# Conditional 1x1 mix plus low-rank update: where TensorE waits in its instruction stream

## The chip, the cores and the metric

The kernel runs on one core of one Trainium2 chip. The metric is the device time of one execution in microseconds (us). Five engines run their own instruction streams and meet only at semaphores: TensorE (PE in the profile; its weight loads are PEld), VectorE (DVE), ScalarE (ACT), GpSimd (POOL) and SyncE (SP), which issues all the transfers here.

## The reference

`x` holds 64 batches of 128 channels by 2048 time steps, in float32. Each batch has a number from 0 to 15 that picks a 128x128 matrix, and a number from 4 to 50 that picks a low-rank adapter.

```python
W = weights[condition]                            # 16 matrices, 128 x 128
x = x + jnp.einsum('bct,bcd->bdt', x, W)          # mix of channels
Bx = jnp.einsum('bni,bri->bnr', x, B[adapter_ids])   # rank 16, over time
out = jnp.einsum('bnr,bor->bno', Bx, A[adapter_ids])
x = x + out                                       # scaling is 1
```

So every batch needs three products: a mix of the channels, a sum over time to rank 16, and a product back to all time steps, with two additions of the input around them.

## The kernel before

A batch is one 128 x 2048 tile. It is worked in four **units** of 512 columns. Batches go in **rounds** of two (`ROUND`), rounds in **turns** of two (`BODY` = 4 batches), so every buffer of a batch exists four times and the two rounds of a turn are of kind 0 and kind 1. 16 turns make 64 batches; turn 0 and the last turn are written out, the 14 between are a hardware loop.

For a batch b the work is:

- POOL adds the identity to the picked matrix (`m_sel`, L215; semaphore `m_picked`), so that the mix gives x + x W at once.
- **mix** (L374): 16 matmuls on PE, one bank of PSUM for each unit; `f_made` counts units. ACT copies each unit out of its bank into `ft` (L262; `copied`).
- **z** (L390): 16 matmuls with 16-column weights from `ab_in` and `ft` as moving data. The four chunks of a unit write four 32-row strips of bank 0 or 1; `z_done` at the end. ACT takes strips 0 and 2 out of the bank, DVE strips 1 and 3 (L269, L309; `z_taken_act`, `z_taken_dve`). POOL adds the four parts, ACT copies the sum to three more groups of rows (`z_placed`).
- **low** (L408): 16 matmuls with 16-row weights from `at`, which DVE makes by transposing half of `ab_in` (L325; `a_turned`). They run in four chunks; a chunk writes 128 columns in each of four banks. `low_done` comes with the last chunk. DVE then adds bank and `ft` for each unit into `x_out` (L316; `added`), and SP stores the tile.

Every matmul in float32 is issued in two pieces, so a stage of 16 matmuls shows 32 pieces in the trace.

PE's order is written out by hand. A round with batches b and b+1 runs mix(b), mix(b+1), z(b), z(b+1), low(b-2), low(b-1). The banks come round: the mix of a round begins in the banks that low of the first batch used in the round before it (`LOW_BANKS`, `F_BANKS`), so its first unit waits for the first `added` of that batch (L371). low of the second batch uses banks 0 and 1, in which z was summed, and so waits for all takes of z(b+1) (L403).

In the kernel before, each stage has its waits in front of its first matmul: `mix_units` at L364 to L371, `sum_z` at L381 to L387, `add_low_rank` at L397 to L404. Where a count depends on the loop's register, the wait is held by a register instruction of its own ahead of the matmul, or by the matmul's first weight load.

The last two batches are written out in another order: mix(62), z(62), low(60), mix(63), low(61), z(63), low(62), low(63). DVE's order at the end is: the adds of batches 58 and 59, the transposes of 62 and 63, the takes of z(62), the adds of 60, and so on.

## Time and profile before

| | us |
|---|---|
| median of 3 runs | 394.99 (393.74 to 397.9) |
| the profiled execution's own time | 394.86 |
| its span, first to last instruction | 393.0 |
| PE busy | 374.7 (95%) |
| PE weight loads busy | 352.8 (90%) |
| ACT busy | 238.5 (61%) |
| DVE busy | 230.2 (59%) |
| POOL busy | 113.2 (29%) |
| share of the DMA queue q1 | 96.3% of 16 engines, 152.19 MB |

Busy time is the time in which at least one instruction of the engine is in work; for PE it includes the stretch in which a matmul drains through the array. The profile also has a chain of waits (who released whom), a timeline, and for each transfer the time from issue to landing.

### The profile page before, as it was taken

How to read it: one execution, taken by the hardware profiler on the slowest of the kernel's cores; microseconds unless marked ns; L12 is line 12 of the kernel's file. 1: busy time of each engine (PE TensorE's matmuls, PEld its weight loads, DVE VectorE, ACT ScalarE, POOL GpSimd, SP SyncE). 2: the span in 40 equal slices, each digit the busy share in tenths (PEclk: the TensorE clock that was granted, in tenths of full speed). 3: DMA queues.
4: the chain of work that ended last, by engine and by line, in shares of the span. 5: the costliest groups of instructions: out<-in, count | busy, mean ns of one | idle time of the engine just before them, and what ended most of it. 6: DMA issues, size and time to landing. Idle time of an engine off the chain costs nothing.

```text
span 393.0 us, 16867 instructions
## 1 busy us (share of the span) xinstructions
PE 374.7 (95%) x6164; PEld 352.8 (90%) x6164; DVE 230.2 (59%) x445; ACT 238.5 (61%) x580; POOL 113.2 (29%) x263
## 2 busy tenths in 40 slices
PE   8789999999999999999999999999999999999971
PEld 8779999999999999999999999999999999999861
DVE  0127655567755556775555677555567765556752
ACT  2366665666666666666666666666666666566541
POOL 1033332223333222333322233332223333222310
PEclk9899999999999999999999999999999999999995
DMA  5998999999999999999999999999999999999547
GB/s 199 402 385 332 379 404 409 408 410 411 412 411 416 410 413 404 417 412 408 413 398 420 409 416 412 407 414 410 413 411 418 404 409 411 416 407 391 243 178 268
DMA packets 28815, 152.37 MB, mean 388 GB/s; under 512 B 3201, under 2 KB 3458, under 8 KB 12546
## 3 DMA queue, kind: packets, MB, share of 16 engines
q1 hardware_dynamic: 28802, 152.19, 96.3%
q8 instruction: 9, 0.15, 0.1%
q14 instruction: 4, 0.03, 0.0%
HBM read 85.07 MB, written 67.11 MB: 387 GB/s over the span
## 4 chain that ended last, share of the span: by engine, by line
PE 92%; DMA 2%; issue 1%; DVE 1%; SPq 1%; ACT 1%; POOL 1%; ACTq 0%; POOLq 0%; DVEq 0%
PE bank L374 59%; PE bank L408 17%; PE bank L390 16%; DMA x_in<-in_x 2%; DVE x_out L316 1%; POOL z_pair L224 0%; DMA ids<-in_ids 0%; DVE z_part L309 0%; SPq L138 0%; ACT x_out L300 0%; ACT z_all L274 0%; SPq L135 0%; SPq L139 0%; POOL z_all L229 0%; ACT ft L262 0%
## 5 line engine op out<-in xcount | busy, mean ns | idle before, releaser
L374 PE MATMUL bank<-m_sel,x_in 128*128 128x128 f32 x2048 | 240.5, 278 | 5.0 <-DMA x_in<-in_x 2.4
L374 PEld LDWEIGHTS bank<-m_sel,x_in 128*128 128x128 f32 x2048 | 233.7, 193 | 10.5 <-DVE x_out L316 3.2
L262 ACT COPY ft<-bank 128x512 f32<-128x512 f32 x256 | 146.0, 586 | 62.4 <-PE bank L374 60.2
L316 DVE TENSOR_TENSOR x_out<-bank,ft 128x512 f32<-128x512 f32 x253 | 154.4, 683 | 21.2 <-PE bank L408 21.2
L224 POOL TENSOR_TENSOR z_pair<-z_part 16x128 f32<-16x128 f32 x128 | 54.8, 444 | 212.8 <-DVE z_part L309 194.5
L309 DVE COPY z_part<-bank 16x128 f32<-16x128 f32 x128 | 36.7, 287 | 119.1 <-PE bank L390 117.1
L274 ACT COPY z_all<-z_all 16x128 f32<-16x128 f32 x192 | 56.9, 296 | 48.8 <-POOL z_all L229 45.8
L408 PE MATMUL bank<-z_all,at 16*128 16x128 f32 x2048 | 69.8, 283 | 2.6 <-DVE x_out L316 2.5
L408 PEld LDWEIGHTS bank<-z_all,at 16*128 16x128 f32 x2048 | 63.3, 188 | 9.7 <-issue 9.5
L390 PE MATMUL bank<-ft,ab_in 128*16 128x128 f32 x2048 | 65.7, 274 | 0.8 <-issue 0.8
L390 PEld LDWEIGHTS bank<-ft,ab_in 128*16 128x16 f32 x2048 | 51.4, 96 | 9.8 <-issue 4.2
L269 ACT COPY z_part<-bank 16x128 f32<-16x128 f32 x128 | 32.8, 256 | 33.6 <-PE bank L390 32.0
L325 DVE STREAM_TRANSPOSE at<-ab_in 128x512 f32<-128x512 f32 x64 | 41.5, 687 | 15.2 <-DMA ab_in<-in_lora 15.2
L215 POOL TENSOR_TENSOR m_sel<-w_all,ident 128x128 f32<-128x128 f32 x62 | 28.3, 456 | 40.4 <-PE bank L374 24.7
L229 POOL TENSOR_TENSOR z_all<-z_pair 16x128 f32<-16x128 f32 x64 | 28.5, 445 | 7.4 <-POOL z_pair L224 4.5
L416 PE MATMUL bank<-ident 128*128 128x128 f32 x20 | 4.6, 429 | 1.6 <-POOL ident L208 1.6
L416 PEld LDWEIGHTS bank<-ident 128*128 128x128 f32 x20 | 4.3, 331 | 1.6 <-POOL ident L208 1.6
L300 ACT COPY x_out<-bank 128x512 f32<-128x512 f32 x3 | 1.6, 594 | 2.3 <-PE bank L408 2.3
L236 POOL TENSOR_TENSOR m_sel<-w_first,ident 128x128 f32<-128x128 f32 x2 | 0.9, 453 | 7.0 <-DMA w_first<-in_weights 7.0
L262 ACT ACT_TABLE_LOAD x1 | 1.3, 1283 | 0.8 <-PEq L468 0.8
L208 POOL TENSOR_SCALAR_AFFINE_SELECT ident<-ident 128x128 f32<-128x128 f32 x1 | 0.3, 292 | 0.2 <-POOL ident L206 0.2
L206 POOL MEMSET ident<- 128x128 f32 x1 | 0.2, 204 | 0.3 <-POOLq L468 0.3
(5 smaller groups left out, 0.4 us busy)
## 6 DMA issues: line engine op xcount, KB each, us to landing
x_in<-in_x SPq DMA_DIRECT2D x63, 1024.0 KB, 11.8
out<-x_out SPq DMA_DIRECT2D x63, 1024.0 KB, 9.9
ab_in<-in_lora SPq DMA_DIRECT2D x64, 256.0 KB, 10.1
w_all<-in_weights SPq DMA_DIRECT2D x1, 1024.0 KB, 8.5
out<-x_out SPq DMA_DIRECT2D x4, 256.0 KB, 4.8
x_in<-in_x SPq DMA_DIRECT2D x2, 256.0 KB, 3.4
x_in<-in_x SPq DMA_DIRECT2D x1, 512.0 KB, 4.6
w_first<-in_weights SPq DMA_DIRECT2D x2, 64.0 KB, 2.7
```

Source lines behind the costliest of these rows:

```text
L215: nc.gpsimd.tensor_tensor(m_sel[k][:], w_all[:, cond, :], ident[:], ALU.add).then_inc(m_picked, 1)
L224: nc.gpsimd.tensor_tensor(z_pair[i][:], parts[2 * i][:], parts[2 * i + 1][:], ALU.add).then_inc(z_paired, 1)
L229: nc.gpsimd.tensor_tensor(z_all[k][rows_of_unit(0), :], z_pair[0][:], z_pair[1][:], ALU.add).then_inc(z_summed, 1)
L262: nc.scalar.copy(ft[k][u][:], bank[f_bank_of(kind, i, u, final)][:]).then_inc(copied, 1)
L269: nc.scalar.copy(z_part[i][c][:], rows_of_z(z_bank, c)).then_inc(z_taken_act, 1)
L274: nc.scalar.copy(z_all[k][rows_of_unit(u), :], z_all[k][rows_of_unit(0), :]).then_inc(z_placed, 1)
L309: nc.vector.tensor_copy(z_part[i][c][:], rows_of_z(z_bank, c)).then_inc(z_taken_dve, 1)
L316: nc.vector.tensor_tensor(x_out[k][:, UNIT * u:UNIT * (u + 1)], bank[banks[u]][:], ft[k][u][:], ALU.add).then_inc(added, 1)
L325: nc.vector.transpose(at[k][:], blocks).then_inc(a_turned, 1)
L374: last = nc.tensor.matmul(to[:, P * c:P * (c + 1)], x_in[k][:, UNIT * u + P * c:UNIT * u + P * (c + 1)], m_sel[k][:], start=(c == 0), stop ...
L390: last = nc.tensor.matmul(rows_of_z(z_bank, c), ab_in[k][:, first:first + RANK], ft[k][u][:, P * c:P * (c + 1)], start=(u == 0), stop=(u = ...
L408: last = nc.tensor.matmul(bank[banks[u]][:, P * c:P * (c + 1)], at[k][rows, js, :].rearrange("r j i -> r (j i)"), z_all[k][rows, :], start ...
```

## The change

Only PE's stream is changed; its matmuls and their order stay. The three stage functions become `mix_unit`, `sum_unit` and `low_chunk`, which hold almost no waits, and five `ask_for_...` functions hold the waits. They are called ahead of the last unit or chunk of a stage for what the next stage needs. Some waits are dropped because another covers them: `ab_loaded` and `z_summed` (covered by `a_turned` and `z_placed`) and two of the waits for `added`.

```diff
-            def sum_z(k, b, turns, z_bank, freed, taken):
-                pe.wait_ge(ab_loaded[k], 16 * turns)
-                pe.wait_ge(copied, UNITS * (b + 1))
-                if live(freed):
-                    pe.wait_ge(added, freed)
-                if live(taken):
-                    pe.wait_ge(z_taken_act, 2 * taken)
-                    pe.wait_ge(z_taken_dve, 2 * taken)
...
-            def add_low_rank(k, b, banks, freed, taken, own=False):
-                pe.wait_ge(a_turned, b + 1)
-                pe.wait_ge(z_summed, b + 1)
-                pe.wait_ge(z_placed, (UNITS - 1) * (b + 1))
-                if live(freed):
-                    pe.wait_ge(added, freed)
-                if live(taken):
-                    pe.wait_ge(z_taken_act, 2 * taken)
-                    pe.wait_ge(z_taken_dve, 2 * taken)
...
+            def ask_for_x(k, b, turns):
+                if isinstance(b, int) and b == 0:
+                    pe.wait_ge(first_loaded[0], 16)
+                else:
+                    pe.wait_ge(x_loaded[k], 16 * (turns - (k == 0)))
+                pe.wait_ge(m_picked, b + 1)
+            def ask_for_ab(b):
+                pe.wait_ge(a_turned, b + 1)
+            def ask_for_ft(b):
+                pe.wait_ge(copied, UNITS * (b + 1))
+            def ask_for_z(b):
+                pe.wait_ge(z_placed, (UNITS - 1) * (b + 1))
+            def ask_for_z_banks(b):
+                pe.wait_ge(z_taken_act, 2 * (b + 1))
+                pe.wait_ge(z_taken_dve, 2 * (b + 1))
...
+            def sum_unit(k, u, b, z_bank):
+                for c in range(IN_UNIT):
+                    first = RANK * (JS + IN_UNIT * u + c)
+                    last = nc.tensor.matmul(bank[z_bank][TILE * c:TILE * c + RANK, 0:P], ab_in[k][:, first:first + RANK],
+                                            ft[k][u][:, P * c:P * (c + 1)], start=(u == 0), stop=(u == UNITS - 1))
+                if u == UNITS - 1:
+                    last.then_inc(z_done, 1)
+            def low_chunk(k, c, banks, own=False):
...
+                if c == IN_UNIT - 1:
+                    last.then_inc(low_done, 1)
...
-                for i in range(ROUND):
-                    mix_units(kind, i, b + i, q + 1, False)
-                for i in range(ROUND):
-                    sum_z(k + i, b + i, q + 1, Z_BANKS[i], UNITS * (b - BODY + 1) + i + 1, b + i - 1)
+                for u in range(UNITS):
+                    mix_unit(kind, 0, u, b)
+                ask_for_x(k + 1, b + 1, q + 1)
+                for u in range(UNITS):
+                    if u == UNITS - 1:
+                        ask_for_ab(b + 1)
+                        ask_for_ft(b)
+                    mix_unit(kind, 1, u, b + 1)
+                if isinstance(b, int) and b == ROUND:
+                    ask_for_z_banks(1)
+                for u in range(UNITS):
+                    if u == UNITS - 1:
+                        ask_for_ft(b + 1)
+                    sum_unit(k, u, b, Z_BANKS[0])
+                for u in range(UNITS):
+                    if u == UNITS - 1 and begun(b - ROUND):
+                        ask_for_z(b - ROUND + 1)
+                    sum_unit(k + 1, u, b + 1, Z_BANKS[1])
                 if begun(b - ROUND):
-                    add_low_rank(other, b - ROUND, LOW_BANKS[kind][0], UNITS * (b - ROUND), 0)
-                    add_low_rank(other + 1, b - ROUND + 1, LOW_BANKS[kind][1], 0, b + ROUND)
+                    for c in range(IN_UNIT):
+                        if c == IN_UNIT - 1:
+                            ask_for_z_banks(b + 1)
+                        low_chunk(other, c, LOW_BANKS[kind][0])
+                    for c in range(IN_UNIT - 1):
+                        low_chunk(other + 1, c, LOW_BANKS[kind][1])
+                ask_for_x(other, b + ROUND, q + 1 + kind)
+                if begun(b - ROUND):
+                    low_chunk(other + 1, IN_UNIT - 1, LOW_BANKS[kind][1])
             def turn(q):
                 for kind in range(KINDS):
                     normal_round(kind, q)
+            ask_for_x(0, 0, 1)
             turn(0)
             with pe.Fori(1, TURNS - 1) as q:
                 turn(q)
             normal_round(0, TURNS - 1)
             b = BATCHES - ROUND
-            mix_units(1, 0, b, TURNS, True)
-            sum_z(ROUND, b, TURNS, Z_BANKS[0], UNITS * (b - BODY + 1) + 1, b - 1)
-            add_low_rank(0, b - 2, LAST_LOW, UNITS * (b - 2), 0)
-            mix_units(1, 1, b + 1, TURNS, True)
-            add_low_rank(1, b - 1, LAST_LOW, UNITS * (b - 1), 0)
-            sum_z(ROUND + 1, b + 1, TURNS, Z_BANKS[0], 0, b + 1)
-            add_low_rank(ROUND, b, LAST_LOW, UNITS * b, 0)
-            add_low_rank(ROUND + 1, b + 1, LAST_OWN, 0, BATCHES, own=True)
+            for u in range(UNITS):
+                if u == UNITS - 1:
+                    ask_for_ab(b)
+                mix_unit(1, 0, u, b, True)
+            ask_for_ft(b)
+            for u in range(UNITS):
+                sum_unit(ROUND, u, b, Z_BANKS[0])
+            ask_for_z(b - 1)
+            for c in range(IN_UNIT):
+                low_chunk(0, c, LAST_LOW)
+            ask_for_x(ROUND + 1, b + 1, TURNS)
+            for u in range(UNITS):
+                mix_unit(1, 1, u, b + 1, True)
+            pe.wait_ge(added, UNITS * (b - 1))
+            for c in range(IN_UNIT):
+                low_chunk(1, c, LAST_LOW)
+            ask_for_ab(b + 1)
+            ask_for_z_banks(b)
+            ask_for_ft(b + 1)
+            for u in range(UNITS):
+                sum_unit(ROUND + 1, u, b + 1, Z_BANKS[0])
+            ask_for_z(b)
+            pe.wait_ge(added, UNITS * b)
+            for c in range(IN_UNIT):
+                low_chunk(ROUND, c, LAST_LOW)
+            ask_for_z(b + 1)
+            ask_for_z_banks(b + 1)
+            for c in range(IN_UNIT):
+                low_chunk(ROUND + 1, c, LAST_OWN, own=True)
```

**Place 1, PE, inside the loop: z and low of a round of kind 0.** Rows are PE's instructions in order (x15: fifteen alike in a row); `REGISTER_ALU` and `ISA` are register instructions that can hold a wait. Before:

```order
L381 REGISTER_ALU [waits ab_loaded1]
L383 REGISTER_ALU [waits copied]
L385 REGISTER_ALU [waits added]
L390 MATMUL bank<-ft,ab_in 16x128 [waits z_taken_dve,z_taken_act]
L390 MATMUL bank<-ft,ab_in 16x128 x15
L398 REGISTER_ALU [waits z_summed,a_turned]
L400 ISA [waits z_placed]
L408 MATMUL bank<-z_all,at 128x128 [waits added]
L408 MATMUL bank<-z_all,at 128x128 x15
L398 REGISTER_ALU [waits z_summed,a_turned]
L402 REGISTER_ALU [waits z_placed]
L408 MATMUL bank<-z_all,at 128x128 [waits z_taken_dve,z_taken_act]
```

With the change, the same stretch from z of the first batch on:

```order
L399 MATMUL bank<-ft,ab_in 16x128 x12
L371 REGISTER_ALU
L399 MATMUL bank<-ft,ab_in 16x128 [waits copied]
L399 MATMUL bank<-ft,ab_in 16x128 x15
L374 REGISTER_ALU
L399 MATMUL bank<-ft,ab_in 16x128 [waits z_placed]
L399 MATMUL bank<-ft,ab_in 16x128 x3
L408 MATMUL bank<-z_all,at 128x128 x12
L377 REGISTER_ALU
L408 MATMUL bank<-z_all,at 128x128 [waits z_taken_dve,z_taken_act]
L408 MATMUL bank<-z_all,at 128x128 x15
L364 REGISTER_ALU [waits x_loaded2]
```

The wait for all copies of b+1 (`copied`) now stands before the last four matmuls of z(b), where it stood behind them. The wait for the takes of z(b+1) now stands before the last four matmuls of low(b-2), where it stood between low(b-2) and low(b-1). The wait for the next x stands before the last chunk of low(b-1).

**Place 2, PE, the end of the program: mix and z of batch 62.** Before:

```order
L374 MATMUL bank<-m_sel,x_in 128x128 [waits copied]
L374 MATMUL bank<-m_sel,x_in 128x128 x3
L390 MATMUL bank<-ft,ab_in 16x128 [waits z_taken_act,added,z_taken_dve,copied,ab_loaded2]
L390 MATMUL bank<-ft,ab_in 16x128 x15
L408 MATMUL bank<-z_all,at 128x128 [waits z_placed,added,z_summed,a_turned]
```

With the change:

```order
L391 MATMUL bank<-m_sel,x_in 128x128 [waits copied,a_turned]
L391 MATMUL bank<-m_sel,x_in 128x128 x3
L399 MATMUL bank<-ft,ab_in 16x128 [waits copied]
L399 MATMUL bank<-ft,ab_in 16x128 x15
L408 MATMUL bank<-z_all,at 128x128 [waits z_placed]
```

The last unit of mix(62) now also waits for DVE's transpose of batch 62; before, z(62) asked only for the loaded adapter.

## Rows read from the trace of the kernel before

**Rows 1.** The page, part 1: busy time, share of the span and count.
```profile
PE 374.7 (95%) x6164; PEld 352.8 (90%) x6164; DVE 230.2 (59%) x445; ACT 238.5 (61%) x580; POOL 113.2 (29%) x263
```
**Rows 2.** Windows: stretch, length, busy and (count) of each engine, clock, DMA, GB/s.
```profile
200.00:240.00 40.00, 39.97 (x720) 37.41 (x718) 23.52 (x48) 25.38 (x63) 12.37 (x29) 1.00 1.01 409
```
**Rows 3.** Timeline, one turn: start us, us, engine, line, op, tiles, count [idle before <-releaser].
```profile
201.64 2.10 PE L390 MATMUL bank<-ft,ab_in 128*16 128x128 f32 x64
201.75 0.59 ACT L262 COPY ft<-bank 128x512 f32<-128x512 f32 x1 [0.31 <-PE bank L374]
202.64 0.81 PEld L390 LDWEIGHTS bank<-ft,ab_in 128*16 128x16 f32 x32 [0.22 <-issue]
...
203.67 2.15 PE L408 MATMUL bank<-z_all,at 16*128 16x128 f32 x64
...
203.89 0.60 DVE L309 COPY z_part<-bank 16x128 f32<-16x128 f32 x2 [0.41 <-PE bank L390]
...
204.98 4.88 DVE L316 TENSOR_TENSOR x_out<-bank,ft 128x512 f32<-128x512 f32 x8 [0.48 <-PE bank L408]
...
205.74 7.41 PE L374 MATMUL bank<-m_sel,x_in 128*128 128x128 f32 x64
...
209.77 1.30 DVE L325 STREAM_TRANSPOSE at<-ab_in 128x512 f32<-128x512 f32 x2
...
213.09 2.00 PE L390 MATMUL bank<-ft,ab_in 128*16 128x128 f32 x64
213.19 0.58 ACT L262 COPY ft<-bank 128x512 f32<-128x512 f32 x1 [0.31 <-PE bank L374]
...
215.02 2.15 PE L408 MATMUL bank<-z_all,at 16*128 16x128 f32 x64
...
215.24 0.60 DVE L309 COPY z_part<-bank 16x128 f32<-16x128 f32 x2 [0.32 <-PE bank L390]
...
216.44 3.68 DVE L316 TENSOR_TENSOR x_out<-bank,ft 128x512 f32<-128x512 f32 x6 [0.60 <-PE bank L408]
...
217.19 2.98 PEld L374 LDWEIGHTS bank<-m_sel,x_in 128*128 128x128 f32 x26 [0.22 <-DVE x_out L316]
```
**Rows 4.** Timeline, three narrow windows: the first low alone, then the second's start.
```profile
203.67 1.17 PE L408 MATMUL bank<-z_all,at 16*128 16x128 f32 x32
...
204.61 0.45 PEld L408 LDWEIGHTS bank<-z_all,at 16*128 16x128 f32 x12
...
204.66 1.15 PE L408 MATMUL bank<-z_all,at 16*128 16x128 f32 x32
```
**Rows 5.** The page, part 5, then who waited for whom from 60 to 345 us.
```profile
L316 DVE TENSOR_TENSOR x_out<-bank,ft 128x512 f32<-128x512 f32 x253 | 154.4, 683 | 21.2 <-PE bank L408 21.2
...
PEld bank L374 <- DVE x_out L316: 2.7, 12, 0.2
```
**Rows 6.** Timeline, the first round, which has no low.
```profile
18.53 1.94 PE L390 MATMUL bank<-ft,ab_in 128*16 128x128 f32 x64
...
20.40 2.75 PEld L374 LDWEIGHTS bank<-m_sel,x_in 128*128 128x128 f32 x24 [0.21 <-issue]
```
**Rows 7.** x transfers from 45 to 55, then 347.5 to 352 us: median us to landing.
```profile
x_in<-in_x SPq DMA_DIRECT2D x2, 1024.0 KB, 8.2
...
x_in<-in_x SPq DMA_DIRECT2D x2, 1024.0 KB, 17.3
```
**Rows 8.** Timeline, the last loads of x and the stages of batch 62.
```profile
348.03 3.02 SPq L128 DMA_DIRECT2D x_in<-in_x  x2
...
365.15 4.88 DVE L316 TENSOR_TENSOR x_out<-bank,ft 128x512 f32<-128x512 f32 x8 [0.56 <-PE bank L408]
...
365.99 3.81 PE L374 MATMUL bank<-m_sel,x_in 128*128 128x128 f32 x32
...
369.89 0.58 ACT L262 COPY ft<-bank 128x512 f32<-128x512 f32 x1 [0.31 <-PE bank L374]
369.94 1.29 DVE L325 STREAM_TRANSPOSE at<-ab_in 128x512 f32<-128x512 f32 x2
370.57 1.26 PE L390 MATMUL bank<-ft,ab_in 128*16 128x128 f32 x32 [0.78 <-issue]
```

55 lines of the change are left out of this document (20 added, 35 removed).

## The prediction, made before the changed kernel ran

> **What bounds the kernel now.** The busy shares come first: PE is busy for 95% of the span, nothing else of the five engines for more than 61% [rows 1]. In the middle of the run PE is busy for 39.97 of 40 us at the full clock of 2.4 GHz, while the DMA engines are busy all the time as well and move 409 GB/s [rows 2]. So there are two candidates, PE and the transfers. The time to landing tells them apart: a load of x takes 8.2 us near 50 us and 17.3 us near 350 us [rows 7]. Transfers fall behind slowly, by about (17.3 - 8.2) / 300 = 0.03 us per us, or 0.35 us in a round of 11.45, so they need some 11.8 us for a round. PE does not wait for them yet: the last pair of x is issued at 348.03, its first tile lands some 17.3 us later, at 365.3, and is needed at 365.99 [rows 7, 8]. PE sets the pace, with 0.6 us in hand at the end.
>
> PE's busy time hides how its stages hang on other engines, so the timeline of one turn comes next [rows 3]. A round is 11.45 us from mix to mix (205.74 to 217.19). At its end stands a chain: the last copy of `ft` by ACT ends (201.75 + 0.59 = 202.34), z of the second batch begins (202.64), DVE's takes of it end (203.89 + 0.60 = 204.49), low of the second batch begins (204.61), and beside that low of the first batch ends (203.67 + 1.17 = 204.84), DVE's first add begins (204.98), and the next mix begins at 205.74 [rows 3, 4]. The gap between the takes' end and the weight load of the second low is 0.12 us in this round, so that wait does end there; the first low has just finished beside it. The question is what the change puts behind these two releases.
>
> **Waits dropped.** `ab_loaded`, `z_summed` and two waits for `added` go. I cost them at nothing. In the round after the first pair, with its conditions long true, the stage change from z to mix has an idle time of 0.21 us [rows 6], and the stage changes in the loop have 0.22 and 0.21 (the second is 203.67 less the last piece of z) [rows 3]. It is about the same at every change of stage, with few waits or many. If a stage change did get cheaper, what follows is still held by the copy and the takes, which don't move.
>
> The page "TensorE: Matmul & The Clock Gate" of the Trainium skill, section "Part 2: What happens when you issue a matmul", says that PE's queue may pull weight loads ahead of matmuls in flight. By that rule a stage that begins without a wait would hide its first weights, and the idle times at the stage changes could go; no row here shows a stage change without a wait. It is a rival below.
>
> **The wait for the copies, moved in front of the last unit of z(b).** Without any hold both z take 1.94 us [rows 6]; in the two rounds of rows 3 they take 2.10 and 2.00. With the change the last quarter of z(b) waits for the last copy. It would start at about 201.64 + 0.66 = 202.30, three quarters through a z of 0.87 (half of 1.94 less the 0.2 in which the last piece drains); the copy ends at 202.34, and release to matmul costs some 0.08. So the hold is 0.12 and both z take about 2.05: 0.05 less than in the one kind of round, 0.05 more than in the other. Sum: nothing.
>
> **The wait for the takes, moved in front of the last chunk of low(b-2).** This is the term that counts. Before, low(b-2) waits for none of them, and all of it runs while DVE empties the banks. Now its last chunk is held until DVE is done at 204.49. From that end to the first matmul behind the wait it is 0.17 us (204.66) [rows 4]. A whole low from there lasts 1.15; the last piece alone takes 0.27, so 32 pieces start within 0.88 and a quarter is 0.22, and one chunk alone lasts 1.15 - 3 x 0.22 = 0.49 [rows 4]. low(b-2) then ends at 204.66 + 0.49 = 205.15, where it ended at 204.84: 0.31 later.
>
> Who waits for it: DVE's adds. The first begins 0.14 after low's end, at 205.29, and takes 0.68 [rows 5], so it ends at 205.97. The next mix writes the bank that this add empties. That wait already ends the idle time of the other kind of round: 216.44 + 0.69 = 217.13, and mix begins at 217.19 [rows 3]; it is the releaser 12 times between 60 and 345 us [rows 5]. So mix begins at 206.03 where it began at 205.74: 0.29 later. PE's own way is no longer: low(b-1) now starts 0.22 to 0.27 later, at about 204.9, has its last piece under way at 205.8, and the stage change of 0.2 gives 206.0. In the other kind: takes end at 215.84, low(b-2) ends at 216.50 instead of 216.19, and the add and the mix move by the same 0.31. Mean of the two: 0.30, from which I take 0.01 for the places where the release is just covered: 0.29 us a round.
>
> The bounds of this term: nothing, if the last chunk's hold were hidden in the next stage as low(b-1)'s is now, and 0.35, if the restart cost the 0.1 between 1.17 and the steady pace again. I take 0.29 because every link of it has a row.
>
> **How often.** Rounds with low are b = 2 to 60: 30. 30 x 0.29 = 8.7 us.
>
> **The waits that are early enough.** The transposes end at 209.77 + 1.30 = 211.07, and the last unit of mix(b+1), which now asks for them, begins at about 205.74 + 7 x 0.90 = 212.0 [rows 3]; both move with the adds. 0.9 us of cover, so nothing. x is asked for 0.2 us earlier than before; with rounds of 11.74 the loads fall behind by 0.06 instead of 0.35 each, and the cover grows. `z_placed` is a round old.
>
> **The end.** Here the wait for the transposes has no cover. mix(62) begins at 365.99 and its last unit, three quarters of 3.65 on, at 368.7. DVE is in its eight adds until about 369.94, and then transposes batch 62 for half of 1.29, to 370.6 [rows 8]. Before, nobody on PE asked for it: z(62) waited for the copy that ends at 370.47 and ran at 370.57. With the change the last unit is held for 370.65 - 368.75 = 1.9 us, and its copy, z(62) and all of PE's stream behind it are later by that. All of it lies on the path, since PE goes on without a break to mix(63). 1.9 us.
>
> **Sum.** 8.7 + 1.9 = 10.6 us on the profiled execution's own 394.86 us gives 405.5. That execution is within 0.2 us of the median of the runs shown (394.99), so it stands for it.
>
> **Rivals.**
>
> - *The hold does not hold* (0.11). Were the takes done before PE comes to the last chunk, only the end's 1.9 and up to 0.1 a round would remain: 395 to 398.8. For it: in the round at 201.64 the takes end 0.35 us before low(b-2) ends, so little is missing. Against: low(b-2) has its last piece under way at 204.84 - 0.27 = 204.57 and comes to its last chunk some 0.13 before that, at 204.44, while after the takes a matmul starts at 204.66 [rows 4]; a restart also lasts 0.09 longer than a chunk in the stream. The case holds from the point at which z(b+1) ends 0.2 us earlier relative to low(b-2), and nothing in the change does that.
> - *Weights come ahead at the stage changes, and the kernel gets faster* (0.03). Its place is z to low and mix to z, with 0.2 us idle each [rows 3], and its price 0.4 x 30 = 12 us at most. For it: the stages start without a wait now. Against: the same 0.21 stands where the conditions were long true [rows 6], and the copy and the takes are the later ones. It would also meet the transfers: x lands only 0.6 us before its use at the end, and the loads are late already, so not more than about 0.6 us of PE's gain there could last, with 1 or 2 us from the first rounds, before the loads fall behind; less the 1.9 of the end the time is 391 to 395, and under 391 only if the loads are less late in other executions. Here belongs what the rule of the skill's page would bring; the trace has it neither proved nor excluded.
> - *The transfers take the pace* (0.07). If a hold costs more than 0.35 us in a round, or loads get slower, x is late, and the last chunk of low(b-1) is held with it, and with that DVE's second four adds. Rounds of 11.85 to 11.9 give 30 x 0.4 = 12 to 14 us and the end 1.9: 408.5 to 410.5.
> - The page "DMA: Bandwidth & Descriptors" of the Trainium skill, section "Specifications", gives about 358 GB/s as what one core gets of HBM. Here the trace disagrees: 409 GB/s for 40 us [rows 2].
>
> My forecast has 0.79, and its own range is 400.5 to 408.5: below it a hold of only 0.13 us a round with the end's 1.9, above it one of 0.35 with a slower restart at the end. As range for the whole I give 400.5 to 408.5; left out are the first two rivals and the top of the third. A change of 1% (3.95 us) is about what a measurement can tell from none. Faster by over 1%, under 391: 0.02, from the second rival. Within 1%: 0.12, the rest of it and the first. Slower: 0.86.
>
> **What would show it.** Right: an idle time of PE within low of the first batch, just behind DVE's takes; low(b-2) from first to last about 1.47 us instead of 1.17; DVE's adds 0.3 us later relative to z; DVE's x_out as releaser of PE's weights for mix in most rounds; rounds of 11.7 us; one wait of some 1.9 us for DVE's transpose at the end; landing times of x that stay near 9 to 11 us. Wrong: a mix that starts as soon after DVE's takes as before (1.25 us), or idle times at z to low that are gone and rounds below 11.4 us; and a wait for x in the loop would show the third rival.

## The result, and the profile after the change

The kernel is slower: 409.68 us (median of 4 runs, 408.0 to 411.12) against 396.44 for the kernel before on the same chip (4 runs, 393.74 to 398.86); the ratio is 1.033 with a 95% interval of 1.025 to 1.042. The profiled execution took 408.0 us with a span of 406.2; before it was 394.86 with 393.0. The range of the prediction, 400.5 to 408.5, just holds the profiled execution and misses the median by 1.2 us. Ratios leave disturbed executions out, while medians and spreads hold all of them.

The page after, part 1 and the clock of part 2: PE is still the busiest engine, with 8.4 us more busy time for the same 6164 instructions. Most of that is in low, whose matmuls are busy for 77.6 us where they were for 69.8: some are held matmuls that count as busy, some run at a slower clock, seen as the 6, 8 and 5 at the end of the row.

```profile
PE 383.1 (94%) x6164; PEld 354.5 (87%) x6164; DVE 230.1 (57%) x445; ACT 240.1 (59%) x580; POOL 113.2 (28%) x263
...
PEclk9999999999999999999999999999999999999685
```

The same 40 us in the middle, as a window (columns as in [rows 2]): PE is busy for 39.80 us where it was for 39.97. Busy time alone would not show the loss: below, low is one unbroken row of PE although its weight loads break for 0.20 us. The counts, 622 where before had 720, are no measure of it either. They hang on where the 40 us begin: before, four pairs of z and low lie in them, after the change three.

```profile
200.00:240.00 40.00, 39.80 (x622) 37.25 (x621) 24.82 (x48) 25.57 (x60) 10.88 (x25) 1.00 1.02 405
```

The timeline of one turn of the loop after the change answers to [rows 3]. L399 is z, L408 is low, L391 is mix:

```profile
205.12 2.03 PE L399 MATMUL bank<-ft,ab_in 128*16 128x128 f32 x64
...
207.08 2.38 PE L408 MATMUL bank<-z_all,at 16*128 16x128 f32 x64
...
207.31 0.61 DVE L309 COPY z_part<-bank 16x128 f32<-16x128 f32 x2 [0.26 <-PE bank L399]
208.03 1.24 PEld L408 LDWEIGHTS bank<-z_all,at 16*128 16x128 f32 x40 [0.20 <-ACT z_part L269]
208.69 4.87 DVE L316 TENSOR_TENSOR x_out<-bank,ft 128x512 f32<-128x512 f32 x8 [0.78 <-PE bank L408]
209.44 7.22 PEld L391 LDWEIGHTS bank<-m_sel,x_in 128*128 128x128 f32 x64 [0.17 <-DVE x_out L316]
...
218.97 0.60 DVE L309 COPY z_part<-bank 16x128 f32<-16x128 f32 x2 [0.27 <-PE bank L399]
219.70 1.24 PEld L408 LDWEIGHTS bank<-z_all,at 16*128 16x128 f32 x40 [0.20 <-ACT z_part L269]
220.47 3.08 DVE L316 TENSOR_TENSOR x_out<-bank,ft 128x512 f32<-128x512 f32 x5 [0.90 <-PE bank L408]
221.22 1.86 PEld L391 LDWEIGHTS bank<-m_sel,x_in 128*128 128x128 f32 x16 [0.29 <-DVE x_out L316]
```

Read it from DVE's takes. They end at 207.31 + 0.61 = 207.92. The weight loads of low now break in the middle, after 24 of 64, and go on at 208.03, 0.11 us behind the takes: this is the last chunk of low(b-2), held. DVE's first add begins 0.77 us behind the takes (208.69), where it was 0.49 before (204.49 to 204.98), and mix begins 1.52 us behind them (209.44), where it was 1.25. In the next round the same two distances are 0.90 and 1.65 (from 219.57), where they were 0.60 and 1.35. The clock is 1.00 in both kernels, so this is waiting. Together with z, which is 0.07 us shorter in the one kind of round and 0.03 longer in the other, this makes rounds of 11.66 and 11.78 us in turn, where both kinds took 11.45. The row's name for the releaser, ACT's z_part, is one of two semaphores waited for there; ACT's and DVE's takes end within 0.1 us of each other.

Who waited for whom from 60 to 355 us (total us, times, longest) answers to the second row of [rows 5]: DVE's x_out was the releaser of mix's weights 12 times for 2.7 us and is now 25 times for 5.7.

```profile
DVE x_out L316 <- PE bank L408: 20.9, 25, 0.9
...
PEld bank L391 <- DVE x_out L316: 5.7, 25, 0.3
PEld bank L408 <- issue: 5.3, 25, 0.2
PEld bank L408 <- ACT z_part L269: 4.9, 25, 0.2
PEld bank L399 <- ACT ft L262: 4.4, 25, 0.2
```

The end of the program answers to [rows 8]. Timeline of PE and of DVE's transpose:

```profile
373.49 2.94 PE L391 MATMUL bank<-m_sel,x_in 128*128 128x128 f32 x24
...
377.54 1.29 DVE L325 STREAM_TRANSPOSE at<-ab_in 128x512 f32<-128x512 f32 x2
...
378.30 1.16 PE L391 MATMUL bank<-m_sel,x_in 128*128 128x128 f32 x8 [1.86 <-DVE at L325]
...
380.18 1.91 PE L399 MATMUL bank<-ft,ab_in 128*16 128x128 f32 x32 [0.73 <-ACT ft L262]
...
382.02 2.09 PE L408 MATMUL bank<-z_all,at 16*128 16x128 f32 x32
...
384.04 4.96 PE L391 MATMUL bank<-m_sel,x_in 128*128 128x128 f32 x32
```

Three quarters of mix(62) run, then PE stands for 1.86 us until DVE has transposed batch 62, and then for 0.73 us for the copy of the held unit. Behind it everything is slow: low of 32 pieces takes 2.09 us where [rows 4] have 1.17, mix(63) 4.96 where mix(62) took 3.81 in [rows 8]. The windows say why (columns as in [rows 2]; behind the length stand the busy times of the five, then the granted clock as a share of 2.4 GHz). After the change:

```profile
376.00:380.00 4.00, 1.60 (x12) 1.22 (x11) 2.83 (x5) 1.28 (x3) 0.00 (x0) 0.95 1.03 426
380.00:384.00 4.00, 3.82 (x64) 2.96 (x64) 0.57 (x2) 0.64 (x3) 1.02 (x3) 0.50 0.26 102
384.00:388.00 4.00, 4.00 (x29) 3.96 (x26) 2.48 (x4) 2.06 (x5) 0.27 (x1) 0.70 0.14 57
```

PE is busy for 1.60 of the 4 us in which the stall lies, and the granted clock is at its lower level, 1.2 GHz (0.50), all through the 4 us behind it, and at 0.70 on average in the next. It was lowered near 379.6, came back near 386.4, and was lowered again from 393.2.

**Where the 13.2 us of span went.** Both traces, cut at the starts of mix:

| stretch | before | after | difference |
|---|---|---|---|
| start to the mix of batches 2 and 3 | 20.40 | 19.07 | -1.3 |
| mix(6) to mix(8), the second round of the first pass through the loop | 11.76 | 13.39 | +1.6 |
| the other 29 rounds up to mix(62) | 333.83 | 341.03 | +7.2 |
| mix(62) to mix(63) | 6.87 | 10.55 | +3.7 |
| mix(63) to the end | 20.19 | 22.18 | +2.0 |
| span | 393.05 | 406.22 | +13.2 |

The first row is chance. In the profiled execution of the kernel before, PE waits 2.36 us for the x of batch 1 and the clock is at its lower level from 14.2 to 17.6 us, so that mix(1) takes 5.46 us. In the changed kernel's PE waits 2.34 us at the same place, the clock stays full and mix(1) takes 3.84. The executions of experiments 1 and 2, with the same code there as the changed kernel, have the lower clock again. The other rows are what the experiments take apart.

### The profile page after: what moved, and what is told of

Its sections match the earlier page's. It is cut to its first block, busy times and chain, and to the rows that moved or that the text cites. A ratio compares the mean times of both kernels' runs of the same rounds, so it can differ in the third digit from the quotient of the medians.

```text
span 406.2 us, 16569 instructions
## 1 busy us (share of the span) xinstructions
PE 383.1 (94%) x6164; PEld 354.5 (87%) x6164; DVE 230.1 (57%) x445; ACT 240.1 (59%) x580; POOL 113.2 (28%) x263
## 4 chain that ended last, share of the span: by engine, by line
PE 87%; DVE 4%; DMA 3%; issue 2%; SPq 1%; ACT 1%; ACTq 0%; DVEq 0%; POOLq 0%; POOL 0%
PE bank L391 56%; PE bank L408 16%; PE bank L399 15%; DVE x_out L316 4%; DMA x_in<-in_x 2%; DMA ids<-in_ids 0%; ACT ft L262 0%; SPq L138 0%; ACT x_out L300 0%; ACT z_all L274 0%; SPq L125 0%; SPq L135 0%; SPq L151 0%; SPq L139 0%; SPq L131 0%
## 5 line engine op out<-in xcount | busy, mean ns | idle before, releaser
L391 PE MATMUL bank<-m_sel,x_in 128*128 128x128 f32 x2048 | 240.0, 278 | 7.2 <-DMA x_in<-in_x 2.8
L391 PEld LDWEIGHTS bank<-m_sel,x_in 128*128 128x128 f32 x2048 | 233.3, 193 | 13.6 <-DVE x_out L316 6.6
L262 ACT COPY ft<-bank 128x512 f32<-128x512 f32 x256 | 147.6, 586 | 69.3 <-PE bank L391 66.6
L408 PE MATMUL bank<-z_all,at 16*128 16x128 f32 x2048 | 77.6, 289 | 4.9 <-DVE x_out L316 2.5
L408 PEld LDWEIGHTS bank<-z_all,at 16*128 16x128 f32 x2048 | 66.2, 192 | 16.9 <-issue 11.1
L399 PE MATMUL bank<-ft,ab_in 128*16 128x128 f32 x2048 | 66.0, 276 | 0.7 <-ACT ft L262 0.7
L399 PEld LDWEIGHTS bank<-ft,ab_in 128*16 128x16 f32 x2048 | 50.7, 97 | 10.6 <-ACT ft L262 6.5
```

Of the source, the lines that this page charges most:

```text
L262: nc.scalar.copy(ft[k][u][:], bank[f_bank_of(kind, i, u, final)][:]).then_inc(copied, 1)
L391: last = nc.tensor.matmul(to[:, P * c:P * (c + 1)], x_in[k][:, UNIT * u + P * c:UNIT * u + P * (c + 1)], m_sel[k][:], start=(c == 0), stop ...
L399: last = nc.tensor.matmul(bank[z_bank][TILE * c:TILE * c + RANK, 0:P], ab_in[k][:, first:first + RANK], ft[k][u][:, P * c:P * (c + 1)], st ...
L408: last = nc.tensor.matmul(bank[banks[u]][:, P * c:P * (c + 1)], at[k][rows, js, :].rearrange("r j i -> r (j i)"), z_all[k][rows, :], start ...
```

## The experiments

Each is timed against the kernel before on its own chip. "After" is the changed kernel.

| experiment | kernel | ratio to before, 95% interval | median us (before) |
|---|---|---|---|
| 1 | after without the hold at the end | 1.0245, 1.0191 to 1.0300 | 405.24 (394.97) |
| 2 | after without the takes' hold | 1.0073, 1.0027 to 1.0119 | 400.27 (394.97) |
| 3 | both | 1.0061, 1.0024 to 1.0097 | 397.34 (394.97) |
| 4 | after, PE kept at work in the stall | 1.0263, 1.0193 to 1.0333 | 406.76 (394.97) |
| 5 | before with the takes' hold alone | 1.0227, 1.0148 to 1.0306 | 403.14 (396.03) |
| 6 | experiment 3 without the copies' hold | 1.0007, 0.9977 to 1.0038 | 396.11 (396.03) |
| 7 | experiment 3, three quarters of z left out | two executions, no interval | 412.93 and 393.8 (394.61) |
| 8 | experiment 3, 10 matmuls more in front of the loop | 0.9994, 0.9958 to 1.0029 | 395.68 (396.03) |
| 9 | before with filling matmuls at two places | 1.0020, 0.9977 to 1.0062 | 396.67 (396.03) |
| 10 | after, 10 matmuls more in front of the loop | 1.0281, 1.0223 to 1.0340 | 406.19 (394.61) |
| 11 | experiment 6, 10 matmuls more in front of the loop | 1.0012, 0.9968 to 1.0055 | 396.46 (394.61) |

### 1. The hold at the end taken away

```diff
             for u in range(UNITS):
-                if u == UNITS - 1:
-                    ask_for_ab(b)
                 mix_unit(1, 0, u, b, True)
+            pe.wait_ge(ab_loaded[ROUND], 16 * TURNS)
+            pe.wait_ge(added, UNITS * (b - BODY + 1) + 1)
             ask_for_ft(b)
...
+            pe.wait_ge(added, UNITS * (b - 2))   # ahead of low(60)
```

The wait for the transposes had covered the two waits for `added` as well, so they come back.

> The changed kernel, but at the end of the program z(62) asks for the loaded adapter again and the last unit of mix(62) no longer asks for DVE's transpose. Theory A (the stall at the end cost its own 2.1 us and then, by the clock that fell to 1.2 GHz at 379.6 us, some 3.5 us more): PE's idle time before the last unit of mix(62) is gone, the granted clock stays at its full level until about 10 us before the span's end as in the kernel before, and the time falls by 5 to 6 us against the changed kernel, to 1.02 of the kernel before. Rival B (only the stall counts and the rest of the end is late for another reason, such as stores or the rounds): the time falls by 2 us, to 1.028 of the kernel before.

Measured: 1.0245, against 1.0334 for the changed kernel. That is 3.5 us less, and the interval leaves room for both theories (1.02 and 1.028); the trace decides. Mix(62) to mix(63) takes 6.76 us, mix(63) to the end 20.24, together 27.00; after the change it was 32.73, before 27.06. The whole 5.7 us are gone, of which only 2.0 were the stall. Mix(62) starts at 376.29 here, and the windows show the full clock around it:

```profile
376.00:380.00 4.00, 4.00 (x44) 3.77 (x37) 4.00 (x8) 2.90 (x8) 0.88 (x3) 1.00 0.35 147
380.00:384.00 4.00, 3.18 (x74) 2.75 (x73) 2.95 (x7) 1.10 (x3) 1.11 (x3) 1.00 0.96 391
```

The rounds stay at 11.72 us: the hold in the loop is untouched.

The span is only 2.9 us shorter than after the change, 403.3 against 406.2, because this execution lost 2.8 us elsewhere: 1.3 in the first two rounds, where its clock is lower for a while, and 1.5 in the round from mix(8). In front of that round PE stands for 1.39 us, as it does in the changed kernel (experiment 3 shows the place), but here the lower clock follows, and mix(8) to mix(10) takes 13.19 us where the changed kernel has 11.66:

```profile
56.00:60.00 4.00, 2.58 (x31) 2.20 (x27) 3.69 (x7) 1.56 (x6) 2.13 (x5) 0.77 1.01 409
```

### 2. The takes' hold taken away

```diff
                     for c in range(IN_UNIT):
-                        if c == IN_UNIT - 1:
-                            ask_for_z_banks(b + 1)
                         low_chunk(other, c, LOW_BANKS[kind][0])
+                    ask_for_z_banks(b + 1)
                     for c in range(IN_UNIT - 1):
```

> The changed kernel, but in the rounds the wait for the takes of z(b+1) stands between the two low products again. Theory A (its place in front of the last chunk is what makes a round 11.72 instead of 11.45 us): rounds of 11.45 us, idle time of PE inside the first low gone, and 30 x 0.27 = 8 us less than the changed kernel, 1.013 of the kernel before. Rival B (the wait for the copies in front of the last unit of z, or the wait for x in front of the last chunk of low, has a share): rounds stay above 11.55 us and the gain is under 5 us.

Measured: 1.0073, and rounds of 11.48 us on average where the changed kernel has 11.72. So this one edit of the order holds the loop's loss. By the ratio 10 us are gone, more than the 8 of theory A, but the executions of this kernel spread from 395.3 to 403.0 us; the size is better taken from the rounds of the trace. The stall at the end is there, as it should be (timeline):

```profile
374.86 1.58 PE L391 MATMUL bank<-m_sel,x_in 128*128 128x128 f32 x8 [1.85 <-DVE at L325]
```

PE has the same two idle times as in the changed kernel, 1.85 and 0.73 us. But the clock is lower for a shorter time here, from 375.4 us, just behind the first of them, to 378.8, and mix(63) takes 3.96 us where the changed kernel has 4.96. Mix(62) to the end takes 30.81 us in this execution, 3.8 more than in experiment 1:

```profile
376.00:380.00 4.00, 3.27 (x67) 2.30 (x65) 0.57 (x2) 1.10 (x3) 0.15 (x1) 0.64 0.45 184
```

New is a wait for x near the end, which the changed kernel never has in the loop:

```profile
358.21 0.50 PE L408 MATMUL bank<-z_all,at 16*128 16x128 f32 x8 [0.44 <-DMA x_in<-in_x]
```

### 3. Both taken away

The changed kernel with the two diffs above and nothing else.

> Both parts moved back: the takes' wait between the two low products, and the end with the waits of the kernel before; the merged waits and all other waits in front of the last matmuls stay. Theory A (these two carry the whole loss, other parts cost nothing): 0.998 to 1.002 of the kernel before, rounds of 11.45 us. Rival B (weights come ahead at stage changes that have no wait): idle times of 0.2 us from mix to z and z to low shrink, 0.98 to 0.99. Rival C (the copies' wait costs too): 1.004 or more.

Measured: 1.0061, rounds of 11.47, mix(62) to the end 27.00. The two holds together account for nearly all of the loss: from 1.033 to 1.006. Some 0.6% remains, more than theory A allowed; by the number rival C came, that the copies' hold costs too, and experiment 6 prices it at 0.09 us a round. The trace shows another thing that before lacks: in the first pass through the loop PE stands still in front of the last chunk of low(b-1) (timeline).

```profile
52.32 1.93 PE L408 MATMUL bank<-z_all,at 16*128 16x128 f32 x56
55.87 0.50 PE L408 MATMUL bank<-z_all,at 16*128 16x128 f32 x8 [1.61 <-issue]
```

The changed kernel has it too, at the same place:

```profile
52.98 2.16 PE L408 MATMUL bank<-z_all,at 16*128 16x128 f32 x56
...
56.52 0.50 PE L408 MATMUL bank<-z_all,at 16*128 16x128 f32 x8 [1.39 <-issue]
```

"issue" says that no semaphore ended it. Near it, a transfer of 16 KB of instructions runs (at 54.0 in the changed kernel; before has it at 51.0, while mix runs). Experiments 8 and 10 take this up.

The same place shows a stall of 1.39 us in experiment 1, 1.60 in 2, 1.12 in 4 and 1.50 in 6. In the executions of experiments 1, 2 and 6 the lower clock follows (from 58.2, 58.0 and 56.2 us) and the next round takes 1.5 to 1.6 us more; in those of the changed kernel and of experiments 3 and 4 it doesn't. So a stall of one length can be followed by a lower clock in one execution and not in another.

### 4. PE kept at work in the stall

```diff
                 if u == UNITS - 1:
+                    pe.wait_ge(copied, UNITS * b + 1)
+                    for _ in range(8):
+                        nc.tensor.matmul(bank[f_bank_of(1, 0, u, True)][:, 0:P], x_in[ROUND][:, 0:P], m_sel[ROUND][:],
+                                         start=True, stop=True, skip_group_check=True)
                     ask_for_ab(b)
```

The wait stays and the stall stays; eight matmuls whose results are overwritten fill most of it. This separates the stall from the clock.

> The changed kernel with eight more matmuls (1.8 us of PE work whose results are overwritten by the unit that follows) in front of the wait for DVE's transpose at the end, where PE sat idle for 2.1 us. The wait and the order of all else stay. Theory A (the idle time itself lowers the clock, and the low clock costs 3.5 us): the last unit of mix(62) starts as late as in the changed kernel, the granted clock stays full through z(62), low(60) and mix(63), and the time falls by 3 to 4 us, to about 1.024 of the kernel before. Rival B (the clock falls anyway in this stretch, or the late end has another cause): no change, 1.033.

The timeline of that kernel (L466 are the added matmuls):

```profile
376.09 1.95 PE L466 MATMUL bank<-m_sel,x_in 128*128 128x128 f32 x16
...
378.11 1.16 PE L391 MATMUL bank<-m_sel,x_in 128*128 128x128 f32 x8
...
380.00 1.07 PE L399 MATMUL bank<-ft,ab_in 128*16 128x128 f32 x32 [0.73 <-ACT ft L262]
381.00 1.17 PE L408 MATMUL bank<-z_all,at 16*128 16x128 f32 x32
382.10 3.94 PE L391 MATMUL bank<-m_sel,x_in 128*128 128x128 f32 x32
```

Z, low and mix(63) take 1.07, 1.17 and 3.94 us where the changed kernel has 1.91, 2.09 and 4.96, and the windows have the full clock until 390.3. Mix(62) to mix(63) is 8.79 = 6.76 (experiment 1) + 2.03: the bare stall. Mix(63) to the end is 21.16 where it was 22.18. So 2.8 us of the end are paid for the clock behind the stall. The 0.9 us that are still paid hang on when the clock falls for the last time: here at 390.3, 13.0 us before the end, in experiment 1 10.6 us before it. Experiments 5 and 11 have no stall at this place and the same 0.9 us (27.8 and 27.9 us from mix(62) to the end, with last falls 12.9 and 13.5 us before it), so they need no stall. The ratio, 1.0263, is by its interval no different from after or from experiment 1; what is said here rests on the trace.

### 5. The takes' hold alone, put into the kernel before

```diff
                 for c in range(IN_UNIT):
+                    if early and c == IN_UNIT - 1:
+                        pe.wait_ge(z_taken_act, 2 * taken)
+                        pe.wait_ge(z_taken_dve, 2 * taken)
...
-                    add_low_rank(other, b - ROUND, LOW_BANKS[kind][0], UNITS * (b - ROUND), 0)
-                    add_low_rank(other + 1, b - ROUND + 1, LOW_BANKS[kind][1], 0, b + ROUND)
+                    add_low_rank(other, b - ROUND, LOW_BANKS[kind][0], UNITS * (b - ROUND), b + ROUND, early=True)
+                    add_low_rank(other + 1, b - ROUND + 1, LOW_BANKS[kind][1], 0, 0)
```

> The kernel before with one part of the change alone: the wait for the takes of z(b+1) stands in front of the last chunk of low(b-2). Theory A (held chunk, later low_done, later first add, later mix): rounds of 11.72 to 11.75 us against 11.45, PE idle inside the first low, 30 x 0.28 = 8.4 us more than the kernel before, 1.021. Rival B (a round is 11.72 only with the other moved waits): under 1.012.

Measured: 1.0227, rounds of 11.71 and 11.74 in turn, 0.28 more than before, as theory A expected. All other waits are those of before, so the hold by itself carries the loop's loss: 30 x 0.28 = 8.4 us, and the ratio says 9.0 (5.9 to 12.1). The timeline shows the same broken low as the changed kernel:

```profile
205.41 2.37 PE L411 MATMUL bank<-z_all,at 16*128 16x128 f32 x64
205.63 0.60 DVE L309 COPY z_part<-bank 16x128 f32<-16x128 f32 x2 [0.41 <-PE bank L390]
206.35 1.24 PEld L411 LDWEIGHTS bank<-z_all,at 16*128 16x128 f32 x40 [0.18 <-ACT z_part L269]
207.01 4.88 DVE L316 TENSOR_TENSOR x_out<-bank,ft 128x512 f32<-128x512 f32 x8 [0.78 <-PE bank L411]
207.75 7.22 PEld L374 LDWEIGHTS bank<-m_sel,x_in 128*128 128x128 f32 x64 [0.17 <-DVE x_out L316]
```

### 6. The copies' hold taken away too

```diff
                 for u in range(UNITS):
-                    if u == UNITS - 1:
-                        ask_for_ft(b + 1)
                     sum_unit(k, u, b, Z_BANKS[0])
+                ask_for_ft(b + 1)
```

> As e3_both, with the wait for the copies of b+1 moved back between z(b) and z(b+1) as well; left of the change are the merged waits, the wait for z_placed in front of the last unit of z, the wait for x in front of the last chunk of low, and the transposes' wait in mix. Theory A (the copies' wait makes one kind of round 0.06 us shorter and the other 0.1 us longer, which nearly cancels): both kinds near 11.45 us and the time within 0.2% of e3_both. Rival B (z to z would gain from the dropped register instructions, since fewer stand between the copy's end and the weight load): rounds of 11.35 to 11.40 and 1.0 to 2.5 us less than e3_both.

Measured: 1.0007. In mid-run the rounds are 11.30 and 11.47 in turn, mean 11.39: 0.07 below before. The copies' hold thus costs 0.09 a round, and what is left of the change gives 0.07. Rival B is the one that came, in the rounds and in the ratio (2.1 us less than experiment 3). Its place can be read: before, the weights of z(b+1) start 0.22 us behind those of z(b) [rows 3], and 0.12 in the other kind of round, with the waits `ab_loaded`, `copied`, `added` and those for the takes between them. Here only `copied` stands there, the last copy ends as early (0.70 us behind the start of z, where before has 0.69), and the weight loads of both z run through without a break, so that both z take 1.94 us:

```profile
201.81 1.66 PEld L399 LDWEIGHTS bank<-ft,ab_in 128*16 128x16 f32 x64
```

Nothing of that reaches the end: x lands 18.6 us after its issue in the window in which [rows 7] have 17.3 for before, and PE waits for it in the last rounds, which take 11.61, 12.12, 11.67 and 12.06 us.

```profile
342.84 0.50 PE L408 MATMUL bank<-z_all,at 16*128 16x128 f32 x8 [0.55 <-DMA x_in<-in_x]
```

### 7. Less work on PE, to find the transfers' own pace

Experiment 3 with only the last of the four units of z computed, so 1536 matmul instructions fewer. Its output is not the reference's.

```diff
             def sum_unit(k, u, b, z_bank):
+                if u < UNITS - 1:
+                    return
```

> As e3_both, but z does only the matmuls of the last unit (three quarters of z is left out, so its output is not the reference's), which takes 0.7 us or more off PE's round while all transfers stay. Theory A (the transfers need 11.6 to 11.9 us a round once they are behind): rounds start at 10.7 us or so, waits for x begin before the middle of the run, rounds are 11.6 to 11.9 us from there on, and the time is 388 to 394 us, hardly less than before. Rival B (the transfers follow at 4.72 MB / 435 GB/s or so = 10.85 us a round): rounds of 10.7 to 10.9 us throughout and 370 to 376 us.

Neither came. One execution took 393.8 us and the profiled one 412.93, with a mean clock of 0.913. In that one the rounds are longer, 11.3 to 13.9 us, because PE now stands at each z for a copy (its weight loads for 0.87 us) and the clock is at its lower level for a part of about every second round:

```profile
200.00:204.00 4.00, 4.00 (x34) 3.77 (x28) 4.00 (x7) 2.34 (x7) 2.22 (x5) 0.50 0.92 368
```

This says nothing about the transfers, and the question of their exact pace stays open. It shows one execution in which PE had less work, with a gap left open in each round, and the kernel took longer than before.

### 8. The same code, 40 instructions later

Ten matmuls of the identity into a free bank, between mix(0) and mix(1) of the first round; PE waits for x there anyway.

```diff
                     mix_unit(kind, 0, u, b)
+                if isinstance(b, int) and b == 0:
+                    for _ in range(10):
+                        nc.tensor.matmul(bank[0][:, 0:P], ident[:], ident[:], start=True, stop=True)
```

> The kernel with both parts moved back (e3_both), and 10 extra matmuls of the identity (40 instructions) between mix(0) and mix(1) of the first round, where PE waits for x anyway. All code of PE behind them lies 40 instructions later. In every kernel with the change PE stands for 1.4 to 1.9 us in its first pass through the loop, ahead of the last chunk of low, without a wait that the profile names, and a 16 KB instruction transfer lies just in front of it. Theory A (the stall is the loading of code, and comes where a boundary of code falls): the stall of the first pass moves or changes in length. Rival B (it belongs to the wait for x and the picked matrix in front of that chunk): it stays where it is, 1.9 us long. For the time: the extra matmuls keep PE busy through the first wait for x, so the clock should not fall there; 0.996 to 1.004 of the kernel before.

Measured: 0.9994, against 1.0061 for experiment 3. The stall of the first pass is gone: low runs as one group, and the round takes 11.84 us where it took 13.47. The instruction transfer is now at 49.9 us, in mix, and not at 53.3.

```profile
53.77 2.15 PE L408 MATMUL bank<-z_all,at 16*128 16x128 f32 x64
56.24 1.94 PE L391 MATMUL bank<-m_sel,x_in 128*128 128x128 f32 x15 [0.32 <-DVE x_out L316]
```

That the stall comes and goes with 40 instructions ahead of it is shown, here and in experiment 10. That PE waits there for its instructions to be loaded is not shown: in experiment 3 the transfer of 16 KB is over at 54.2 us, about when the stall begins. This is the fastest version of the study and no different from before.

### 9. The kernel before, with its idle places filled

The same ten matmuls, and eleven more between z(63) and low(62) behind a wait for the first add, to keep PE at work where before had its own fall of the clock (from 382.8 us).

```diff
+                    if isinstance(b, int) and b == 0 and i == 1:
+                        fill(0, 10)
                     mix_units(kind, i, b + i, q + 1, False)
...
             sum_z(ROUND + 1, b + 1, TURNS, Z_BANKS[0], 0, b + 1)
+            pe.wait_ge(added, UNITS * (b - 1) + 1)
+            fill(LAST_LOW[0], 11)
             add_low_rank(ROUND, b, LAST_LOW, UNITS * b, 0)
```

> The kernel before with extra matmuls of the identity in two stretches in which PE sits idle: 10 between mix(0) and mix(1) in the first round, and 11 between z(63) and low(62) at the end, into a bank that is free there. Theory A (the clock falls behind an idle stretch of some 2.6 us, and the matmuls behind it pay for it): the granted clock stays full from 7 us on to the last matmul, the end is 0.8 to 1 us shorter, the start up to 1.7 us, together 1 to 2.5 us less, 0.994 to 0.998 of the kernel before. Rival B (the idle stretches don't set the clock at these places, or the extra matmuls delay the waiting ones): 1.000 or more.

Measured: 1.0020, no gain, a miss for the expectation that a full clock is worth time. The clock is full from 7.0 to 385.9 us. But the last rounds wait for x, which lands 19.0 us after its issue:

```profile
365.77 3.84 PE L374 MATMUL bank<-m_sel,x_in 128*128 128x128 f32 x32 [1.02 <-DMA x_in<-in_x]
```

What PE gained at the start, the transfers took back at the end.

### 10. The changed kernel, 40 instructions later

The diff of experiment 8, put into the changed kernel.

> The changed kernel as it is, with the 10 extra matmuls of e9_pad between mix(0) and mix(1) of the first round. Theory A (1.4 us of the loss is the loading of code at a boundary that the change put in front of the last chunk of low): the stall of the first pass shrinks from 1.66 us to about 0.3 over a normal change of stage, as in e9_pad, and the time falls by 1 to 2 us against the changed kernel, to 1.028 to 1.031 of the kernel before. Rival B (the place of the boundary is not what counts): stall and time stay, 1.033.

Measured: 1.0281 (1.0223 to 1.0340) against 1.0334 for the changed kernel. The first pass's stall is gone there too (PE's longest idle time there is 0.41 us, the round 12.09 instead of 13.39), rounds and end are as they were (11.72; mix(62) to mix(63) 10.50). The trace gives this 1.3 us; the two ratios differ by that much, but less than their intervals.

### 11. Experiment 6, 40 instructions later

The diff of experiment 8, put into the kernel of experiment 6.

> The kernel with all three harmful or neutral waits moved back (e6_all) and the 10 extra matmuls, so without the stall of the first pass: PE's rounds are 11.385 us against 11.455 before, so PE alone would be 30 x 0.07 = 2.1 us faster. Theory A (the transfers need more than 11.455 us a round and had 0.6 us in hand at the end of the kernel before): waits for x appear in the last rounds, the rounds there are 11.6 to 12.1 us, and the time is that of the kernel before within 0.5% (0.995 to 1.002). Rival B (the transfers follow): 0.993 to 0.995, no wait for x.

Measured: 1.0012. No stall in the first pass, rounds of 11.30 and 11.47 in mid-run, and then 11.85, 12.62 and 12.44 among the last with waits for x (from 300 to 385 us):

```profile
PE bank L408 <- DMA x_in<-in_x: 2.2, 3, 1.0
```

So both versions with rounds of 11.39 us give the gain back to the transfers.

## Why the prediction was right and where it was wrong

**The hold in the loop: right, in place and size.** Predicted was 0.29 us a round, 8.7 in all, by the chain from the takes' end over low's last chunk and DVE's add to mix. Measured are 0.27 in the changed kernel and 0.28 for the hold alone (experiment 5); taking it away gives it back (experiments 2 and 3). Over the whole run the rounds lost 7.5 us: some 0.27 in 29 of the rounds, while the one from mix(2) got 0.2 shorter. The single links hold as well: 0.11 us from takes to weights, low(b-2) from first to last 1.47 us (207.08 to 0.14 before the add at 208.69), add 0.28 later against the takes, mix 0.27 later.

**The hold at the end: mechanism right, price wrong. This is the step that failed.** The term was 1.9 us, and the stall measures 2.0. But the prediction put z(62), low(60) and mix(63) behind the stall at the speed that they had before; the clock was a term of nothing, without a reason given. PE's idle 1.86 us and then 0.73 us came with the lower clock, from 379.6 us on, and mix(62) to the end lost 5.7 us, not 1.9. Experiment 1 gives back all of it. Experiments 1 and 4 split it: 2.0 for the stall, 2.8 for the clock behind it, and 0.9 for an earlier last fall of the clock, which other executions have without a stall. Nor is 5.7 a fixed price: the same stall cost 3.8 us in the execution of experiment 2 and 6.0 in that of experiment 10. The 3.8 us missed here are more than the whole miss of the profiled execution (408.0 against 405.5).

The trace of before had the hint. PE had waited for x at the start and for DVE's adds near the end; its clock was lower from 14.2 and from 382.8 us, and mix(1) took 5.46 us. Timeline and windows of before:

```profile
13.14 5.46 PE L374 MATMUL bank<-m_sel,x_in 128*128 128x128 f32 x32 [2.36 <-DMA x_in<-in_x]
...
381.42 3.20 PE L408 MATMUL bank<-z_all,at 16*128 16x128 f32 x64 [2.53 <-DVE x_out L316]
...
12.00:16.00 4.00, 2.86 (x17) 2.87 (x18) 1.38 (x2) 0.59 (x1) 0.00 (x0) 0.77 1.03 429
380.00:384.00 4.00, 2.53 (x60) 2.40 (x64) 2.55 (x5) 0.89 (x3) 1.30 (x3) 0.85 0.51 209
```

**How far off the time was.** Part of the median's miss is not the prediction's: it added 10.6 us to an execution of 394.86, and the kernel before had a median of 396.44 this time. The difference of the medians is 13.2, and the forecast as a ratio, 1.027, lies within the measured interval of 1.025 to 1.042. So the times alone would not tell the price of the end from 1.9; the traces do.

**The dropped waits: nothing, as predicted, but by cancellation.** The prediction had z(b+1) held by the last copy. But the copy ends at 202.33, before the last weights of z(b) are loaded (202.43), and the weights of z(b+1) follow only at 202.64. With the waits dropped that gap closes (experiment 6), and the round is 0.07 us shorter; the copies' hold takes 0.09, and where the gain is not taken by the hold it is taken by the transfers. The waits for the takes ahead of z went too, which the list of dropped waits leaves out. The prediction also counted a change from mix to z at 0.22 us: that row of [rows 3] lies between z(b) and z(b+1), and from mix to z weight loads are idle for 0.12. Both z take 2.03 us, where 2.05 was foreseen.

**The transposes and x in the loop: right.** No row of a wait for either stands in the loop. x lands after 8.1 us between 340 and 352 us, where before had 17.3 [rows 7]. The prediction had transfers needing 11.8 us a round and falling behind by 0.06 even in slower rounds. In this execution they kept up with 11.72 entirely. That doesn't make 11.8 too high: with the same rounds the landing time between 340 and 352 us is 9.3 in experiment 4, 10.2 in 10, 12.2 in 5 and 12.7 in 1, up from 8.0 to 8.4 near 50 us in each. The first row is after the change, the second experiment 1:

```profile
x_in<-in_x SPq DMA_DIRECT2D x2, 1024.0 KB, 8.1
...
x_in<-in_x SPq DMA_DIRECT2D x2, 1024.0 KB, 12.7
```

**Not foreseen: the first pass.** 1.3 us or so for a stall that comes and goes with 40 instructions ahead of it, and 1.5 us more in executions in which the clock falls behind it. No term stood for it. In this pair of executions it is offset by the luckier start.

**The rivals.** That the hold does not hold is excluded by the broken low. Its price was also summed about 1 us too low: 394.86 + 1.9 and up to 3 for the rounds is 396.8 to 399.8. That weights come ahead at the changes from z to low and from mix to z is excluded by rows of the changed kernel: z to low has no wait now, and 0.21 us of idle weight loads as before ("PEld bank L408 <- issue: 5.3, 25, 0.2" above); from mix to z it is 0.12 in both kernels. Between the two z it is otherwise: there the idle time goes when the waits are dropped (experiment 6), a place that the rival had not named. The Trainium skill, page "TensorE: Matmul & The Clock Gate", section "Part 2: What happens when you issue a matmul", says that the queue may pull weight loads ahead of matmuls in flight; at the changes from mix to z and from z to low the trace doesn't show it doing so. The transfers took the pace in no round of the changed kernel, only in the faster versions.

**The sum in the end.** The start gave -1.3 (chance), the round of the first pass 1.6 (1.3 for its stall, 0.3 for the hold), the other rounds 7.2, the end 5.7: 13.2 us of span, against 10.6 predicted. So the loop was 1.2 us cheaper than forecast (7.5 for 8.7) and the end 3.8 dearer, and the two terms that nobody had cancel by luck.

## What to carry to other kernels

A wait moved ahead of the last piece of a stage is free only if it is met by then, or if that piece has no reader on the path. Here the stage's end releases another engine, which releases the next stage, so all of the hold comes out at the end of the round. Follow the reader of the held piece before counting what the earlier wait saves.

A stall is to be priced twice: its length, and what the clock may cost behind it. In this kernel a stall of 2 us cost 3.8, 5.7 and 6.0 us in three executions.

Where PE and the transfers are nearly balanced, look at the landing times over the run before promising a gain. Landing times that grow from 8 to 17 us say that less work on PE will turn into waiting for x.

## What the runs showed of the hardware that was not expected

- PE idle for 1.86 us and again for 0.73 us came with 1.2 GHz from 379.6, in the second idle time, to 386.4. In experiment 2, with the same idle times, it was from 375.4, behind the first, to 378.8. In the kernel before, 0.78 us idle near 370 alone was not followed by a lower clock. Matmuls without a use, in the stall, kept the clock at full until 390.3 (experiment 4).
- A stall of 1.1 to 1.6 us in the first pass through a loop came in six kernels and was gone with 40 more instructions ahead of it (experiments 3 and 8, after and 10). In three of the six executions the clock fell behind it, in three it didn't.
- From z to low PE's weight loads are idle for 0.21 us, from mix to z for 0.12, in the kernel before with its waits and in the changed kernels without one there. Between two z it was 0.22 or 0.12 us with all the waits of before, and nothing with one (experiment 6).
- With rounds of 11.39 to 11.48 us, at about 410 GB/s, transfers fall behind slowly and land after 17 to 19 us instead of 8. With rounds of 11.72, at about 400 GB/s, they land after 8 to 13 us, and the executions differ.
